# A two-layer transformer-like kernel: where the second routing's slot owners and the first expert weight loads stand

## The reference, cut to what matters

```python
xn = _layernorm(x)
# attention of layer 1: a linear projection, then FFTs of length 256
query, keys, values = (unit_projection(xn @ W.T + b) for W, b in ...)   # f / (|f| + 1e-8)
x_k = bind(keys, values)            # product of spectra
s = cumsum(x_k, axis=1)
s = unbind(s, query)                # product with the conjugate spectrum, back to real
# feed-forward of layer 1: 8 experts, each token goes to 2
gate_scores = softmax(xn @ Wg + bg)
topk_scores, topk_idx = top_k(gate_scores, 2)
g = silu(sum over e of (gelu(xn @ W1[e] + b1[e]) @ W2[e] + b2[e]) * combine_w[..., e:e + 1])
x = x + s * g
```

## Time and profile before

| | us |
|---|---|
| median of 3 runs | 1121.63 |
| lowest and highest | 1120.66, 1124.16 |
| the profiled execution's own time | 1117.8 |
| its span | 1115.8 |
| granted TensorE clock, mean over the span | 0.968 of full |

### The profile page before, as it was taken

One profiled execution on the slowest core, in us unless ns is written; L12 is line 12 of the kernel. 1 busy time (PEld: TensorE's weight loads), 2 busy tenths in 40 slices (PEclk: granted clock), 3 DMA queues, 4 the chain that ended last, 5 costly groups with the idle time before them and its releaser, 6 DMA issues.

```text
span 1115.8 us, 16806 instructions
## 1 busy us (share of the span) xinstructions
PE 1026.7 (92%) x6152; PEld 886.4 (79%) x6152; DVE 688.6 (62%) x1490; ACT 532.2 (48%) x1102; POOL 418.1 (37%) x391
## 2 busy tenths in 40 slices
PE   3867899999999994979999999999999999999994
PEld 2655788888888873668889998988888888888884
DVE  6796777777777767687846644474676100148753
ACT  3633754555545536733454545455353222356531
POOL 1056545554455452200243322332331345432273
PEclk9988999999999996987999999999999999999998
DMA  9932245445565428525497754544344679899961
GB/s 301 283 141 86 81 124 189 153 153 180 163 193 190 126 89 275 184 95 249 103 350 260 291 204 180 203 166 156 110 168 154 241 265 343 320 336 389 392 256 55
DMA packets 120402, 228.65 MB, mean 205 GB/s; under 512 B 14939, under 2 KB 103915, under 8 KB 115329
## 3 DMA queue, kind: packets, MB, share of 16 engines
q1 hardware_dynamic: 106448, 189.31, 48.7%
q0 software_dynamic: 13872, 38.27, 10.4%
HBM read 166.98 MB, written 62.79 MB: 206 GB/s over the span
## 4 chain that ended last, share of the span: by engine, by line
PE 74%; DVE 12%; ACT 4%; issue 3%; DMA 3%; POOL 2%; SPq 0%; POOLq 0%; DVEq 0%; ACTq 0%
PE PS L1314 21%; PE PS L1324 20%; PE PS L1213 6%; PE PS L1048 4%; PE PS L1098 3%; PE PS L1152 3%; PE PS L1223 2%; PE PS L1179 2%; PE PS L1107 2%; POOL table L2335 2%; PE PS L1165 2%; PE PS L1190 2%; DVE stats L1355 1%; PE PS L1300 1%; PE PS L1289 1%
## 5 line engine op out<-in xcount | busy, mean ns | idle before, releaser
L2292 ACT ACTIVATE hT<-PS,WE 128x256 f32<-128x256 f32 (+1 forms) x312 | 141.0, 454 | 255.2 <-PE PS L1314 240.1
L1314 PE MATMUL PS<-xgT,WE 128*128 128x256 f32 (+1 forms) x1248 | 253.3, 361 | 2.6 <-ACT hT L2292 1.8
L1324 PE MATMUL PS<-WE,hT 128*128 128x256 f32 x1104 | 244.6, 379 | 0.0
L1314 PEld LDWEIGHTS PS<-xgT,WE 128*128 128x128 f32 x1248 | 219.4, 190 | 29.4 <-ACT hT L2292 2.5
L1324 PEld LDWEIGHTS PS<-WE,hT 128*128 128x128 f32 x1104 | 207.4, 190 | 26.9
L1951 DVE TENSOR_TENSOR y<-PS,WE 128x512 f32<-128x512 f32 (+1 forms) x38 | 24.3, 640 | 206.9 <-PE PS L1324 201.7
L2410 POOL DMA_INDIRECT result<-y,result_of x53 | 53.8, 1016 | 175.8 <-DVE y L1951 168.6
L2398 POOL DMA_INDIRECT xg<-xn_dram,token_of x71 | 74.3, 1046 | 90.7 <-DVE result_of L1867 68.7
L1048 PE MATMUL PS<-XT,Wf 128*128 128x256 f32 x384 | 93.4, 399 | 3.3 <-ACT Z L2069 3.3
L1048 PEld LDWEIGHTS PS<-XT,Wf 128*128 128x128 f32 x384 | 75.1, 201 | 15.3 <-ACT Z L2069 4.9
L2351 POOL TENSOR_TENSOR prob<-prob,row_sum 128x512 f32<-128x512 f32 x56 | 58.6, 1046 | 59.8 <-DVE row_sum L1531 59.1
(11 more groups left out here) (280 smaller groups left out, 1711.9 us busy)
## 6 DMA issues: line engine op xcount, KB each, us to landing
WE<-in_experts SPq DMA_DIRECT2D x39, 2180.0 KB
wgu<-in_w_gate SPq DMA_DIRECT2D x32, 256.0 KB
wgu<-in_w_up SPq DMA_DIRECT2D x32, 256.0 KB
wdn<-in_w_down SPq DMA_DIRECT2D x32, 256.0 KB
result<-zeros SPq DMA_DIRECT2D x16, 512.0 KB
xs<-late_dram SPq DMA_DIRECT2D x16, 512.0 KB, 12.9
both<-result SPq DMA_DIRECT2D x16, 512.0 KB
table<-zeros POOLq DMA_DIRECT2D x1, 5160.0 KB, 31.2
```

Source lines behind the costliest of these rows:

```text
L1314: m = e.matmul(PS[:, FIRST_H_BANK + nth % HR, 0:rows], W1[n % WR][:, k, c * P:(c + 1) * P], xgT[:, n % 2, k, 0:rows], start=k == 0, stop=k ...
L1324: m = e.matmul(PS[:, u.bank, j * D:(j + 1) * D], hT[:, n % 2, c, j * P:(j + 1) * P], W2[n % WR][:, c, :], start=c == 0, stop=c == KF - 1)
L2292: e.activation(hT[:, n % 2, c, 0:rows], PS[:, FIRST_H_BANK + (KF * n + c) % HR, 0:rows], ACT.Gelu_apprx_tanh, bias=b1[n % WR][:, c:c + 1], ...
```

## The change

The item `owners` and the three items `load_weights 0` to `2` move in the list: from ahead of the tables and behind table group 1 to behind `gelu_table`, which follows the eighth group, `first_sum 2` and `magnitudes 2`, and stands right ahead of `rows_found`. And `some(1)` stands behind groups 1, 2, 4 and 6 instead of 2 and 4. No instruction is added or dropped.

```diff
@@ -523,16 +523,12 @@
     add("route1_count")
     some(5)
     add("route1_slots")
-    for n in range(WR):
-        add("load_weights", n)
     for i in range(len(ROW_GROUPS)):
         add("rows_of", i)
         if i == 1:
-            add("owners")
-        if i == 1:
             add("squares", 0)
             add("squares", 1)
-        if i in (2, 4):
+        if i in (1, 2, 4, 6):
             some(1)
         if i == 4:
             for ch in range(2):
@@ -543,6 +539,9 @@
     add("first_sum", 2)
     add("magnitudes", 2)
     add("gelu_table")
+    add("owners")
+    for n in range(WR):
+        add("load_weights", n)
     add("rows_found")
     for n in range(XR):
         add("load_rows1", n)
```

## The result

The changed kernel takes 1133.01 us (median of 6 runs, 1128.95 to 1136.4) against 1121.47 for the kernel before: a ratio of 1.010, 95% interval 1.0081 to 1.0118. It is slower, as forecast, but by 11.5 us where 6.9 were named: above the forecast's own 1126 to 1130.5, and above 1132, the top of the range over all cases. The profiled execution took 1133.03 us, its span 1131.0 against 1115.8.

What follows compares the result with a forecast made beforehand. VectorE's chain ahead of `w2 1` was taken as the bound. Tables and owners 0, chunk 7's save +6.9, clock 0: 1121.63 becomes 1128.5, own range 1126 to 1130.5, over all cases 1118 to 1132.

Steps and rivals of the forecast that it cites:

- The bound: VectorE's chain (bind 0, bind 1, emptying of `w2 0`'s bank), not TensorE, is what `w2 1` waits for from 533.84 on.
- Tables and owners: Table groups and owners' block ahead of `rows_found`: 0 on the deciding chain, only placing `owner_ready` at 523.6.
- The landing: Chunk 7's save behind the weight loads in SP's queue: lands at 545.4, VectorE's first `PR` write 6.9 us later.
- The upper bound of +8.4: Upper side of the save's delay, if the gathers take twice their share of the DMA engines.
- `w1 0`: Start of the block loop on TensorE: waits for the first weights, about 532, some 2 us before 533.92.
- Two spectra fewer ahead of `nyq`: TensorE ahead of `nyq`: 3.5 us less at full clock, a gain taken alone, not on the deciding chain.
- A: Chunk 7's save passes between the weights' packets, landing near 533; gain of 2 to 4 us, at best 1118; chance 0.20.
- B: Among the tables the clock stays up, owners come early: `owner_ready` 520.0, landing 541.8, +3.3, 1124.9; chance 0.15.
- C: TensorE's new holes cost clock: `w1 1` at half clock hides in part, `w2 1` doesn't; +10.4, 1132; chance 0.12.
- The hole of 4 us ahead of `inverse 0`: TensorE was to idle some 4 us ahead of `inverse 0`, and 3 in the rest.
- D: No change: owners early and a smaller save's share, or `w2 1` late anyway; within 1 us, 1121.6; chance 0.08.

## Why the prediction was right in direction and wrong in size

*The bound.* Right: what decides `w2 1` is VectorE's chain, and its new wait is for chunk 7's save behind the weights. Shown by the row at 552.50, by two loads put in front of the save in the kernel before (+0.96% with owners and first weights early) and by the save put ahead (+0.34% instead of +1.0%).

*Tables and owners.* Right: the owners' 3 us behind the tables (521.52 to 524.50) lie beside the wait for the last product, and 2.07 us of it are left ahead of `rows_found`. Against the tables' start `owner_ready` came at 31.95 us where 33.2 were named (524.50 and 492.55 against 523.6 and 490.36).

*The landing* is the term that was mis-sized, and it is nearly all of the miss. The forecast added 17.3 us for the loads, 1.8 for the save, 1.5 for five gathers and 0.2: 20.8 from the first load's issue. Measured are 26.8, 26.3 and 26.8. Added up from the GB/s column, the loads with seven gathers (7.6 MB) were through some 21 us behind the first issue, where the forecast had 18.8 with five; this is an estimate that takes the save to come last, and the stretch at 272 to 284 GB/s is in it. The save with its tail took the rest, nearly 6 us instead of 2.0, because the sum treated 16 engines as one pipe: the save counts as landed when the last of its pieces is, and the bulk was through 3 us before that. With 4.4 MB of loads in front (and chunk 6's save, 0.8 MB, issued 1.4 us ahead of them) the landing was still 23.4 us behind the first of them (529.24 to about 552.6, its issue at 533.04 and 19.6), with 2.2 MB 11.5. The upper bound of +8.4 allowed only for the gathers, not for that tail.

*The sum again.* In the first profile of the changed kernel 6.9 were forecast; the landing adds 6.0, the earlier owners take 1.3, and 1.3 are lost behind `w2 1`: 12.9 us, against 13.0 between the two spans once the later start of 2.2 is taken off. The medians differ by 11.5.

*`w1 0`* was named at 532 and came at 541.12. The forecast took the first weights as what it would wait for; it was the gathered rows, issued behind the start of the loads and slow beside them (6.81 us of idle). Then it started at half clock (9.41 us in all instead of 7.17). It was hidden here, since `w2 0` ended at 557.87 just as bind 0 did, but it would have kept `w2 1` from starting before about 565.5 even with no save in the way (541.12 and the 24.4 us from `w1 0` to `w2 1` in the two runs where TensorE alone set it, 534.40 to 558.77 and 538.85 to 563.27). The forecast had 563.2 for `w2 1` and held this path to be shorter.

*Two spectra fewer ahead of `nyq`* was called a gain taken alone. It is a loss of 0.2% (1.0006 to 1.0037): those spectra filled the time in which the rows come in, and with them in place the clock was at 1.00 when `w1 0` began.

*Rivals.* A (the save is let through) is ruled out. B fell too: the clock still dropped among the tables (group 1's product took 3.66 us at 498.66). C named a real cost, half clock behind a hole. In the first profile it lies only ahead of `w1 0`, and `w2 1` ran at full clock behind 1.84 us of idle (7.17 us). In the second profile of the same kernel it is where C had it:

```profile
568.43 8.86 PE L1323 MATMUL PS<-WE,hT 128*128 128x256 f32 x32 [2.08 <-DVE y L1950]
```

The granted clock fell to 0.50 from 570 to 572 there, and `w2 1` took 1.7 us more, half of C's price. The hole of 4 us ahead of `inverse 0` that C shares with the forecast didn't come, as `w1 0` was so late; it is there in the runs with late loads alone and with two loads in front of the save (5.69 and 5.38 us), and `w1 1` took 9.09 and 8.89 us behind it instead of 7.07. So C's +3.5 was added to a landing that was too short, but it isn't refuted. D falls with the ratio. The page of the Trainium skill cited for B ("TensorE: Matmul & The Clock Gate", section "Part 1: The HAM clock gate") says that activity releases the throttle. The traces agree: the clock stood at 0.50 behind the hole ahead of `w1 0` and came back to 1.00 while `w1 0` ran (546 in the first profile). But the spectra moved were activity taken from a place that needed it more.

**Still open:** why the DMA queue slows down some 17 us into the loads and why one engine or so ends its part of the save 2 to 3 us behind the others. Neither fewer gathers nor the small save explains it. And no run issues the save from another engine's queue, so it isn't shown how much of the delay is the order within SP's queue and how much the sharing of the DMA engines. One pair of rows speaks for the order: the second gather, from GpSimd's queue, was in 8.7 us behind its issue at 530.61, the save issued at 531.19 took 21.1; but the gather is only a sixth of its size. No version tried beats the kernel before.

## What to carry to other kernels

A transfer that a chain without slack waits for should not stand behind a bulk load in the same queue; when a load is moved, list what is behind it in that queue and who waits for its landing, and price that by the last piece of it, not by the mean rate. Before matmuls are moved away from a place where TensorE would otherwise wait for rows, count the clock: here the work behind the hole began at half clock, and the hole plus that price ate the gain. Look, too, at what else such a move lets go early: in the run with six spectra early it was a small save in tiny pieces, and the gathers behind it were late.

## What the runs showed of the hardware beyond what was expected

A queued save of 768 KB lands 3.2 to 4.6 us behind its issue when nothing is in front, 5.8 with one load of 2180 KB (issued 5.7 us earlier), and 19.6 to 22.6 with two or three begun 3.8 to 9.4 us earlier (24.2 for the one issued 3.5 us behind the first of three). Small gathers on another queue (128 KB each) are slowed by bulk loads too: the second gather's rows reached TensorE 8.7 us behind its issue at 530.61, against less than 5 in the kernel before (issue at 528.05, TensorE at 532.59 without a wait). With no load beside it but a save of only 64 KB in pieces of 16 bytes issued 1 us ahead, the same gather took 7.15 us. And behind idle times of 2.47 to 7.67 us ahead of `w1 0` the granted clock was 0.50 at its start and its 32 matmuls took 8.65 to 9.56 us instead of 7.17, in every run that had such an idle. Shorter ones went both ways: `w2 1` kept its clock behind 1.84 us (7.17 us) and lost it behind 1.91 to 2.08 us (8.86 us in three profiles).
